# Scores of the first query tile: two matmuls over side-by-side keys in place of three, with the second part added by VectorE

## The reference, cut to what matters

```python
logits = jnp.einsum('bhtd,bhds->bhts', q, k) * scale
mask = jnp.triu(jnp.full((t, t), -jnp.inf, dtype=x.dtype), k=1)
weights = jax.nn.softmax(logits + mask, axis=-1)
out = jnp.einsum('bhts,bhsd->bhtd', weights, v)
```

## Time and profile before

| what | value |
|---|---|
| median of 3 runs | 1551.54 us (1551.46 to 1552.58) |
| the profiled execution | 1555.36 us, span 1553.5 us |
| PE busy | 1514.6 us (97%) |
| DVE busy | 995.0 us (64%) |
| ACT busy | 735.1 us (47%) |
| granted TensorE clock, mean | 0.993 |
| attention | about 364 to 1050 us of the span |

### The profile page before, as it was taken

The page is one execution under the profiler, slowest core; times in us unless marked ns, Lnnn a source line. Parts: engine busy times, 40 slices in busy tenths (PEclk is TensorE's granted clock), DMA queues, the critical chain, the costliest instruction groups (busy, mean ns, idle before and its releaser), DMA issues.

```text
span 1553.5 us, 29329 instructions
## 1 busy us (share of the span) xinstructions
PE 1514.6 (97%) x8844; PEld 1350.2 (87%) x8844; DVE 995.0 (64%) x2216; ACT 735.1 (47%) x1743; POOL 721.9 (46%) x769
## 2 busy tenths in 40 slices
PE   8899999998999999999999999999999999999998
PEld 4678778887899999999999999988989999999986
DVE  6877666666777777777777777774467322222268
ACT  3542222245666666666666666663332233333332
POOL 2113333346666566666565765679713211111064
PEclk9899999999999999999999999999999999999999
DMA  8235655567848575666657484744333556656365
GB/s 295 109 124 185 214 196 190 205 238 270 259 148 256 175 220 179 215 194 193 210 165 234 146 248 151 235 170 177 132 115 141 189 196 234 262 197 255 132 197 176
DMA packets 203295, 304.05 MB, mean 196 GB/s; under 512 B 80384, under 2 KB 142208, under 8 KB 196048
## 3 DMA queue, kind: packets, MB, share of 16 engines
q1 hardware_dynamic: 196096, 281.80, 53.2%
q0 software_dynamic: 5680, 18.62, 4.0%
q10 hardware_dynamic: 1440, 2.62, 0.5%
HBM read 187.35 MB, written 115.64 MB: 195 GB/s over the span
## 4 chain that ended last, share of the span: by engine, by line
PE 87%; DVE 3%; POOL 3%; DMA 3%; issue 2%; ACT 1%; another core or an unknown queue 0%; SPq 0%; POOLq 0%; ACTq 0%; DVEq 0%
PE bank L1576 47%; PE bank L1672 17%; PE bank L1787 7%; PE bank L1739 7%; PE bank L1770 4%; PE bank L1837 2%; PE bank L1873 1%; PE bank L1590 1%; DMA xin<-ffn_rows 1%; POOL h L1240 1%; POOL acc L1232 1%; DMA acc<-wmod 1%; DMA w<-experts_lo 1%; POOL xr L1240 0%; DVE row_max L2225 0%
## 5 line engine op out<-in xcount | busy, mean ns | idle before, releaser
L1576 PE MATMUL bank<-w,xt_hi 128*128 (+2 forms) x1136 | 283.1, 331 | 6.2 <-DVE xt_lo L2201 3.0
L1576 PEld LDWEIGHTS bank<-w,xt_hi 128*128 128x128 f32 x1136 | 198.0, 190 | 13.0 <-DVE xt_lo L2201 3.4
L1576 PE MATMUL bank<-w,xt_lo 128*128 (+2 forms) x568 | 184.5, 325 | 0.0
L1400 ACT ACTIVATE prob<-prob,row_inv 128x128 f32<-128x128 f32 (+3 forms) x256 | 137.3, 560 | 79.3 <-DVE row_inv L2238 79.1
L2355 DVE TENSOR_TENSOR ht_lo<-bank,ht_hi 128x128 fp32r<-128x128 f32 (+1 forms) x213 | 48.3, 282 | 180.0 <-ACT ht_hi L1517 176.3
L1388 ACT ACTIVATE prob<-bank,neg_max 128x128 f32<-128x128 f32 (+3 forms) x256 | 133.5, 525 | 42.3 <-DVE neg_max L2230 42.1
L1576 PE MATMUL bank<-wv_hi,h_hi 128*128 128x256 f32 x512 | 147.1, 287 | 0.0
L1576 PE MATMUL bank<-w,ht_hi 128*128 (+3 forms) x426 | 140.5, 411 | 6.5 <-DVE ht_lo L2355 5.1
L1576 PE MATMUL bank<-wv_hi,h_lo 128*128 128x256 f32 x512 | 144.8, 283 | 0.0
L1576 PE MATMUL bank<-wv_lo,h_hi 128*128 128x256 f32 x512 | 144.7, 283 | 0.0
L980 POOL CAST q_hi<-q_raw 128x512 fp32r<-128x512 f32 x62 | 68.9, 1111 | 123.8 <-PE bank L1739 114.0
(11 more groups left out here) (249 smaller groups left out, 4148.1 us busy)
## 6 DMA issues: line engine op xcount, KB each, us to landing
keys<-k_ring SPq DMA_DIRECT2D x64, 512.0 KB, 3.0
ch_raw<-wexp SPq DMA_DIRECT2D x128, 170.0 KB, 3.0
experts_hi<-ch_hi SPq DMA_DIRECT2D x128, 170.0 KB, 2.5
experts_lo<-ch_lo SPq DMA_DIRECT2D x128, 170.0 KB, 2.7
w<-experts_hi SPq DMA_DIRECT2D x10, 2176.0 KB, 7.9
w<-experts_lo SPq DMA_DIRECT2D x10, 2176.0 KB, 14.5
q_transposed<-q_out SPq DMA_DIRECT2D x64, 256.0 KB, 2.0
k_even<-keys SPq DMA_DIRECT2D x16, 1024.0 KB, 5.7
```

The costliest lines, as they stand in the source:

```text
L1400: ins = act.activation(part, part, ACT.Copy, scale=row_inv[:, h, r:r + 1])
L1576: ins = pe.matmul(dst, a, m, start=(k == 0), stop=(k == last))
```

## The change

For query tile 0 the three matmuls of 128 columns become two. The first has `q_hi` as weights and moves 256 columns, the hi and the lo keys of tile 0 side by side; its output goes to columns 0 to 127 (hi by hi) and 384 to 511 (hi by lo) of the bank. The second, `q_lo` by the hi keys, adds onto columns 0 to 127. DVE then adds the causal mask to columns 384 to 511 and puts the sum into SBUF (`masks[:, 0, :]`), waits for it, and adds `masks` (this sum for tile 0, a copy of the causal mask for tile 1) to both diagonal blocks. The copy of the causal mask is made once, ahead of the attention.

```diff
+        masks = sbuf(s2, "masks", [P, 2, P])
...
+                    to = bank[s_bank(i, first and m is n)]
                     for r in rows:
...
+                        dst = to[:, at:at + w]
+                        if r == 0:
+                            both = to[:, :].rearrange("p (k n) -> p k n", n=P)[:, 0:4:3, :]
+                            pe.matmul(both, q_hi[:, h, 0:P], k_both[s][:, :, h, 0:P], start=True, stop=True)
+                            pe.matmul(dst, q_lo[:, h, 0:P], k_both[s][:, 0, h, 0:P], start=False, stop=True,
+                                      skip_group_check=True)
+                            continue
...
             stage1_over(dve)
+            link(dve.tensor_copy(masks[:, 1, :], causal[:, :]))
...
                     if len(rows) == 2:
+                        dve.tensor_tensor(masks[:, 0, :], at_bank[:, 3 * P:4 * P], causal[:, :],
+                                          ALU.add).then_inc(s_mask, 1)
+                        dve.wait_ge(s_mask, m * 8 + (i // 3 * 4 + 1))
                         diag = at_bank[:, 0:3 * P].rearrange("p (k n) -> p k n", k=3)[:, 0:3:2, :]
-                        mask = causal[:, :].unsqueeze(1).to_broadcast([P, 2, P])
+                        mask = masks[:, :, :]
...
                     dve.tensor_tensor(diag, diag, mask, ALU.add).then_inc(s_mask, 1)
-                    dve.wait_ge(s_mask, m * 6 + (i + 1))
+                    dve.wait_ge(s_mask, m * 8 + (i + 2 + i // 3))
```

More of the change, by code:

```diff
@@ L1736, in scores @@
                         at = ROW_AT[r] - ROW_AT[rows[0]]
-                        dst = bank[s_bank(i, first and m is n)][:, at:at + w]
+                        dst = to[:, at:at + w]
[5 more added lines that the diff above has]
+                            continue
                         for k, (a, key) in enumerate(((q_hi, 0), (q_hi, 1), (q_lo, 0))):
```

## The result

The changed kernel takes 1568.62 us, median of 5 runs (1567.81 to 1570.56), against 1551.46 us before on the same chip (5 runs). The ratio is 1.0111, 95% interval 1.0100 to 1.0123: slower by 17 us where 6.8 were forecast. In the profiled executions the spans differ by 13.2 us only, 1566.7 against 1553.5, because the one of before is 3.8 us above its median of 1551.54; up to turn(1) of the last step (1053.14 against 1034.70 us) the difference is 18.4.

A forecast was written before the change was run, and what follows sets the result against it. A slackless DVE and ACT chain was taken to bound project(1) to turn(1), PE the rest of each step. 32 x 0.31 - 31 x 0.10 = +6.8 us on 1551.54 gave 1558.3 us, range 1554.2 to 1562.5.

The forecast's parts named there:

- the bound: Between project(1) and turn(1) a DVE and ACT chain as long as PE's work, no slack; PE bounds the rest.
- the sum for a usual step: Chain to turn(1) +0.31 us, PE's scores(0) of the next step -0.10: a usual step grows by 0.21 us.
- part 0 is covered: The other head's 0.31 us on DVE hides in 0.41 us while ACT is busy with o_hi; costed at nothing.
- Nothing there has a pause that would take up a delay, so what lengthens maxima(3) lengthens the whole: DVE and ACT chain from add(1) to normalise(5): pieces back to back, so the 0.31 us added counts in full.
- slow split output: Rival, chance 0.10: PE's wide matmul with output in two pieces takes 0.22 or 0.23 us, no saving; 1561.4 us.
- early mask: Rival, chance 0.08: part 3's mask starts as much earlier as scores(3) end; chain grows only 0.21 us, 1555.1 us.
- The range: Whole kernel: 1554.2 to 1562.5 us, taking in early mask and slow output, leaving out the faster case.

The follow-up runs named there:

- dve_only: Kernel before plus only the new DVE add (result unused) and its wait, three matmuls kept; 1571.68 us, ratio 1.0139.
- pe_only: Kernel before with only PE's two matmuls for query tile 0 of both heads, DVE as before; 1548.26 us, ratio 0.9965.
- a_split: Changed kernel with the two-element -scale written as two one-element operations; 1558.09 us, ratio 1.0032 to the kernel before.
- a_narrow: Changed kernel with GpSimd's ch_lo computed for 16 of 340 columns, DVE untouched; 1559.11 us, ratio 1.0056 to the kernel before.
- a_between: Changed kernel with invert(2) moved between the new add and the mask of part 3; 1557.72 us, ratio 1.0043 to the kernel before.
- b_split: Kernel before with the two-element -scale written as two one-element operations; 1551.54 us, ratio 0.9989.
- head0: Kernel before with the whole change for head 0 (part 0) alone, head 1 as before; 1549.06 us, ratio 0.9974.
- dve_split: Kernel before with DVE's part of the change alone, as dve_only, plus the -scale as two one-element operations; 1608.49 us, ratio 1.0376.

## Why the prediction was wrong

**Right: the bound.** Turn(1) waits in every step after, on the chain from add(1) over maxima(3) to normalise(5). dve_only makes each usual step 0.30 longer without touching PE. The mask stands 0.40 behind invert(2) there, 0.08 before, so of 0.32 added hardly 0.02 found slack.

**Right, with sizes a little off: the sum for a usual step.** Forecast +0.31 for the chain and -0.10 for PE, measured +0.30 (dve_only) and -0.12 (pe_only, 21.09 to 20.97), together 21.27, not 21.30. The add 0.27, the wait behind it 0.04, the mask 0.01 earlier: invert(2) at 655.47, the add 0.07 behind it. Had all steps been so, the change would have cost 31 x 0.18 = 5.6 us, and the time would have been near 1557; a_split, a_narrow and a_between took 1557.7 to 1559.1. The cleanest test is a_split against b_split, the change without collisions on either side, on one chip: 1558.09 - 1551.54 = 6.6 us, where 6.8 were forecast.

**Right: part 0 is covered.** Even 0.31 and a collision of 0.7 on top, more than the 0.41 of cover that the prediction read, lengthened no step (head0).

**Wrong: "Nothing there has a pause that would take up a delay, so what lengthens maxima(3) lengthens the whole", taken as if each piece kept its length.** The step that failed is the costing of a delay as a pure shift of pieces with fixed durations. One piece, the -scale of 0.17 us, has a length that depends on when it begins against GpSimd: in 13 steps of the kernel before it began 0.25 ahead of `ch_lo`, less than the 0.31 that the change was to add, and behind its start it took 0.91. The Trainium skill, SBUF — State Buffer, "Who interferes with whom", has a mechanism for it: VectorE's two-port modes and GpSimd share a pair of ports, whoever issues first has it for the whole instruction, and the other is fully blocked. For DVE behind GpSimd the traces agree: 0.91 us behind `ch_lo` of 0.92, 1.40 behind `q_lo` of 1.56, 0.17 when 0.03 ahead. The Trainium skill, VectorE: DVE Perf Modes, "Mode 2×_2P", says that this mode splits the operand in half along its outermost dimension and reads each half through a port of its own. One element a row has no halves, and none of the 253 one-element operations in a_split was over 156 ns; that the ports are the reason no trace shows, only which form is blocked and for how long.

What it cost: 14 steps x (22.00 - 21.27) = 10.2 us, seen in the traces, and 3.1 of the 3.9 us by which turn(1) of step 1 comes later (the -scale takes 1.04, 1.49, 2.17 and 1.05 us in the steps up to there; in a_split this turn(1) is 3.1 earlier). From turn(1) of step 1 to that of step 31 the whole is 14.5 us: 10.2, and 30 x 0.18 = 5.4, less 1.1 for step 2, which had its collision before too.

The trace of before gave the hint in the view that the earlier trace rows are from, DVE's groups by form (here of 370 to 1100 us), and in step 2 the operation itself at 1.40 us.

```profile
L2230 DVE TENSOR_SCALAR neg_max<-row_max 128x2 f32<-128x2 f32 x63 | 17.1, 272 | 2.1
```

A mean of 272 ns for an operation whose rows show 170 says that some are far longer; most of these are of part 0, some 0.65 us long behind a `q_lo` and under cover. Of the rivals none was this one. The slow split output fell (each part (0, 1) is 0.10 shorter on PE); the sentence of the Trainium skill, PSUM — Partial Sum Buffer, Specifications (TRN2), on access patterns that aren't contiguous is not borne out for an output of two runs of 128 columns. The early mask fell: it came 0.01 earlier, not 0.10.

**The range** was made of bounds of two prices. It had no term for a change of phase between engines, and 10 us lay there, with 3 more in the start.

## What to carry to other kernels

A delay on a chain is not only added, it changes what each operation on it meets: before costing a shift, put GpSimd's operations beside DVE's small ones from SBUF to SBUF that have more than one element a row, and read how far each is from the start of one (of DVE's forms only two elements and one were tested here). Such tiny operations are cheap to make safe: one element at a time cost 0.02 to 0.03 us a step here and took away delays of 0.7 to 1.2. And where a chain and an engine are equally long, make a trade between them only where the chain has cover: for head 0 alone the same change gave 0.26%, part of it by luck.

## What was not expected of the hardware

A loop of DVE can stop for 8 us at its back edge (8.22 us at 474 us in dve_split), and one instruction more ahead of the loop takes the stops away. The Trainium skill, Runtime: NRT & Kernel Launch, "Instruction fetch mechanics", says that crossing a block of 256 instructions is mostly hidden, and warns that a taken branch to a block that isn't loaded must wait for a fetch. The stops agree with the warning, though no trace shows what was fetched; they cost 49 us at six back edges (1608.49 against 1559.17). An edit of the code ahead of a loop can have this effect, so where a time jumps by tens of us the count of instruction packets is worth a look first.
